# Two attentions: the products with the values move ahead of the projections in TensorE's order

## The reference, cut to what matters

```python
def cross_attention(x, ctx, wq, wk, wv, wo, bo):
    q = einsum('bne,ef->bnf', x, wq)      # 20 heads of 64
    k = einsum('bme,ef->bmf', ctx, wk)
    v = einsum('bme,ef->bmf', ctx, wv)
    scores = einsum('bhnd,bhmd->bhnm', q, k) * 64 ** -0.5
    attn = softmax(scores)
    out = einsum('bhnm,bhmd->bhnd', attn, v)
    return einsum('bnf,fe->bne', out, wo) + bo

x = cross_attention(layer_norm(x), layer_norm(x), ...) + x   # "self"
x = cross_attention(layer_norm(x), context, ...) + x         # "cross"
```

## Time and profile before

| | |
|---|---|
| median of 3 runs | 1538.18 us (1535.44 to 1538.56) |
| profiled execution, its own time | 1541.71 us |
| its span, first to last instruction | 1539.9 us |
| TensorE busy | 1384.9 us (90%) |
| DVE, ACT, POOL busy | 1077.4, 756.4, 723.1 us |
| mean granted TensorE clock | 0.959 of full speed |

### The profile page before, as it was taken

The page is one execution under the profiler, slowest core; times in us unless marked ns, Lnnn a source line. Parts: engine busy times, 40 slices in busy tenths (PEclk is TensorE's granted clock), DMA queues, the critical chain, the costliest instruction groups (busy, mean ns, idle before and its releaser), DMA issues. The chain is left out here.

```text
span 1539.9 us, 39601 instructions
## 1 busy us (share of the span) xinstructions
PE 1384.9 (90%) x16544; PEld 1183.2 (77%) x16544; DVE 1077.4 (70%) x2019; ACT 756.4 (49%) x1389; POOL 723.1 (47%) x514
## 2 busy tenths in 40 slices
PE   4697689997699999999979999999999999998587
PEld 3574477875588888888966888888888888887477
DVE  2774678884777778777647776767777777764476
ACT  0442357764355455554534555555555554544243
POOL 1242157675643344433433555555555554556154
PEclk9999889997799999999987999999999999999699
DMA  4110000000200000000010000000010000000000
GB/s 103 52 39 1 21 7 12 5 2 1 63 2 2 2 2 2 2 2 2 2 38 6 2 7 2 7 2 7 2 40 3 1 2 2 2 2 2 13 14 21
DMA packets 23484, 19.25 MB, mean 12 GB/s; under 512 B 12950, under 2 KB 21722, under 8 KB 23322
## 3 DMA queue, kind: packets, MB, share of 16 engines
q1 hardware_dynamic: 23322, 16.89, 4.1%
HBM read 15.57 MB, written 1.31 MB: 11 GB/s over the span
## 5 line engine op out<-in xcount | busy, mean ns | idle before, releaser
L492 POOL TENSOR_TENSOR cross_probs_l<-cross_probs 128x1024 f16<-128x1024 f32 x160 | 303.6, 1898 | 276.3 <-ACT cross_probs L563 276.0
L563 ACT ACTIVATE cross_probs<-cross_score 128x1024 f32<-128x1024 f32 x160 | 164.0, 1025 | 249.8 <-PE cross_score L805 249.8
L492 POOL TENSOR_TENSOR self_probs_l<-self_probs 128x1024 f16<-128x1024 f32 x80 | 151.5, 1894 | 204.1 <-ACT self_probs L563 203.7
L660 DVE TENSOR_REDUCE cross_maxima<-cross_max 128x2 f32<-128x1024 f32 x160 | 194.7, 1217 | 7.4 <-PE cross_max L781 7.2
L1971 POOL TENSOR_TENSOR ad_probs_l<-ad_probs 128x1024 f16<-128x1024 f32 x64 | 121.1, 1893 | 89.3 <-ACT ad_probs L2028 89.0
L563 ACT ACTIVATE self_probs<-self_score 128x1024 f32<-128x1024 f32 x80 | 82.3, 1028 | 156.7 <-PE self_score L805 156.7
L825 PEld LDWEIGHTS cross_pv<-cross_v_h,cross_probs 128*128 128x128 bf16 x1280 | 116.5, 98 | 33.2 <-issue 28.2
L825 PE MATMUL cross_pv<-cross_v_h,cross_probs 128*128 128x65 bf16 x1280 | 135.2, 196 | 2.6 <-POOL cross_probs_l L492 2.6
L646 DVE TENSOR_TENSOR cross_qk_l<-cross_shared,cross_qk_h 128x256 fp32r<-128x256 f32 (+1 forms) x160 | 87.9, 556 | 69.0 <-ACT cross_qk_h L548 68.8
L826 PE MATMUL cross_pv<-cross_v_l,cross_probs 128*128 128x64 f16 x1280 | 133.8, 194 | 0.0
L827 PE MATMUL cross_pv<-cross_v_h,cross_probs_l 128*128 128x65 bf16 x1280 | 133.4, 193 | 0.0
(11 more groups left out here) (439 smaller groups left out, 4806.6 us busy)
## 6 DMA issues: line engine op xcount, KB each, us to landing
ad_ctx_rows<-in_ctx SPq DMA_DIRECT2D x8, 192.0 KB, 2.5
cross_ctx_rows<-in_ctx SPq DMA_DIRECT2D x8, 192.0 KB, 2.7
x_rows<-in_x SPq DMA_DIRECT2D x1, 1280.0 KB, 6.9
sw_raw<-in_L_xattn_wq SPq DMA_DIRECT2D x2, 640.0 KB, 6.1
sw_raw<-in_L_xattn_wk SPq DMA_DIRECT2D x2, 640.0 KB, 3.5
sw_raw<-in_L_xattn_wv SPq DMA_DIRECT2D x2, 640.0 KB, 3.8
cw_raw<-in_L_xattn_wq SPq DMA_DIRECT2D x2, 640.0 KB, 4.1
lr_raw<-in_L_xattn_w_ff SPq DMA_DIRECT2D x2, 640.0 KB
```

What stands on the lines that cost most here:

```text
L492: nc.gpsimd.tensor_tensor(probs_l[:, n % PR, :, :].rearrange("p j k -> p (j k)"), whole, whole.bitcast(BF16)[:, 1::2], ALU.subtract).then_ ...
L563: nc.scalar.activation(probs[:, n % PR, :, :].rearrange("p j k -> p (j k)"), score_bank[:, :], ACT.Exp, scale=SCALE).then_inc(exped, 1)
L660: nc.vector.reduce_max(out, scores, AX.X).then_inc(max_read, 1)
```

## The change

It reorders one list. In each round the groups of `weigh` stand first, directly behind maxima and scores, and the shared items follow. Their own order, and so the ring of shared banks, the order on ACT, DVE and POOL, and every wait's count, stay as they are.

```diff
--- before.py
+++ after.py
@@ -319,18 +319,21 @@
         cur, more = kind != "tail", extras(kind, s)
         last = ROUNDS - 1
         out = []
+        weigh = (s >= WEIGH and cur) or (s < WEIGH and kind != "first")
+        if cross:
+            out += [(0, ("weigh", group)) for group in (0, 1) if weigh]
+        else:
+            out += [(0, ("weigh", group)) for group in range(4) if weigh]
         if (s >= MT and cur) or (s < MT and kind != "first"):
             out.append((0, ("mt", s)))
         out += [(0, key) for key in more[:2] if cross]
-        weigh = (s >= WEIGH and cur) or (s < WEIGH and kind != "first")
         if cross:
-            out += [(0, ("weigh", group)) for group in (0, 1) if weigh]
+            out += [(last, ("weigh", group)) for group in (2, 3) if weigh]
         if cur:
             out.append((last, ("proj", s)))
             if cross:
                 out.append((last, ("kproj", s)))
         out += [(last, key) for key in (more[2:] if cross else more)]
-        out += [(last, ("weigh", group)) for group in ((2, 3) if cross else range(4)) if weigh]
         return out
```

## The result

The changed kernel took 1655.49 us, the median of 4 runs (1651.77 to 1657.88), against 1538.37 (1535.44 to 1539.98, 4 runs) for the kernel before on the same chip. The ratio is 1.0761 [1.0736, 1.0787]. The forecast was 1659, so the time lies 3.5 us from it and on the side that was given 0.96.

What follows compares the result with a forecast made beforehand. TensorE's own order was taken as the bound (busy 47.3 of 48.1 us per self batch, 75.2 of 75.8 cross). Cross +60.7, self +62.0, changing kinds -2 gave 121: 1541.7 became 1663, less 3.5 hence 1659 us; range 1625 to 1695.

Steps and rivals of the forecast that it cites:

- The path: Last shared item on TensorE, ACT's cast, DVE's low part, reciprocal, multiplication, up to the multiplication's end: 2.28 us.
- The ordinary wait: In an ordinary slot of either attention, TensorE's next products wait 0.72 us for DVE's multiplication.
- The waits of cross: New TensorE waits summed over the cross-attention's slots: 64.3 us, 63 of them at 0.72.
- Slots with statistics: Slot 1, self and cross, statistics in front of the reciprocal: wait 1.52 us, six times in each attention.
- cross slot 4: Slot with `ln` work on ACT and DVE: 8.2 us against some 6.9 of TensorE's, wait 1.3, six times.
- the steady waits on maxima in cross fall away: Waits of 0.6 us in each of six cross batches, 3.6 in all, were to vanish.
- The waits of self: New TensorE waits summed over the self-attention's slots: 71.5 us, 35 of them at 0.72.
- Slot 3: Self slot with the normalisation on DVE: grows from 3.84 to 6.17 us, wait 2.33, six times.
- What goes: Old waits to vanish: cross maxima 3.6 us; self bank wait 4.0 and small stalls in slot 8 and at `ot` 5.5.
- Changing between kinds: TensorE's switches between matmul kinds, 240 rounds: products into a projection 0.08 us; together about -2 us, bounds -24 and +22.
- Rival 3: TensorE's clock falls at waits in self slots 3 and 4: 6 to 31 us more, middle 1675; chance 0.20.
- Rivals 1 and 2: First: no wait arises, order cheaper, 1525 us, chance 0.03; second: only slow slots pay, 1579 us, chance 0.05.

Runs made afterwards that it cites:

- x3: Changed kernel, but DVE does the reciprocal and multiplication right behind the slot's last reduction of maxima; 1532.78 us, ratio 0.9981 to the kernel before.
- x5: Changed kernel plus one unread DVE reduction in each slot ahead of the wait for `pv_done`; 1733.73 us, ratio 1.1281 to the kernel before.
- x6: Kernel before plus one unread DVE reduction in each slot ahead of the wait for `pv_done`; 1554.16 us, ratio 1.0114.
- cross alone: New order in the cross-attention only, self as in the kernel before; 1589.77 us, ratio 1.0354 to the kernel before.

## Why the prediction was right

**The mechanism.** It was that the last act of DVE's slot comes due earlier on TensorE while the path to it stays. x3 takes it off the path and with it the whole loss; x5 lengthens the path and pays 78 us of the 87 that 160 times 0.54 can be, where x6 pays 18. The hand-over of 0.15 us came out so in the slots shown (0.15, 0.16, 0.10). The path was right (2.29 against 2.28). The ordinary wait reads 0.67 us in the rows and not 0.72, since a row counts from the scores' modelled end, 1.44 us behind the maxima's start, and the forecast from the next instruction's start, 1.38 behind it. In time the forecast stands: the same cross slot lasts 7.77 us from product to product in x3, which has no wait (1000.13 to 1007.90), and 8.48 in after (1091.46 to 1099.94), 0.71 more.

**The signs** that the prediction named came out thus: a cross batch of 82.7 us for about 84, a self batch of 55.7 to 57.4 for about 57, the longest wait in self 2.3 for 2.4, idle time up by 110 us for some 120. The clock leaving 1.00 in the attentions was named as a sign of being wrong, and in self it did leave it; what that cost stands below.

**The waits of cross**, forecast at 64.3 us, were 54.1 (49.8 on DVE and 4.3 in the tail slots on POOL). Slots with statistics wait 1.46 (forecast 1.52). The term that failed is cross slot 4, "wait 1.3, six times" (its own terms, 2.4, 1.15 and 4.74, make 8.3 and not 8.2, so even 1.4), and with it "the steady waits on maxima in cross fall away". Timeline of the changed kernel, behind that slot:

```profile
1138.20 1.02 DVE L649 TENSOR_TENSOR cross_qk_l<-cross_shared,cross_qk_h 128x256 fp32r<-128x256 f32 x2
1138.31 0.49 PE L784 MATMUL cross_max<-cross_qk_h 64*128 64x512 f32 x2 [0.81 <-DVE cross_maxima L663]
```

I had laid these waits at the second maxima of slot 4. They are at the first maxima of slot 5, whose bank waits for the reduction that stands behind the `ln` work on DVE, and were 0.60 each before. So the delay of slot 4 is mostly paid there, where 0.60 was already being paid; the products behind it wait only 0.10. The forecast had 6 x (1.3 - 0.60) = 4.2 us for the two places together, and they cost 6 x (0.10 + 0.81 - 0.60) = 1.9. The total on maxima went from 6.7 to 8.3, where it was to fall by 3.6. The cross stage grew by 51.2 us where 60.7 were forecast (cross alone, by its median, 54.6). Slot 4 explains 2.3 of that. Idle time grew by 54.2 us, and TensorE's busy time in cross fell by 3.0; what the changes between kinds and the short spells of low clock at the stage's start have in this, no run takes apart.

**The waits of self**, forecast at 71.5, were 62.6. Slot 4 waits 2.29 (forecast 2.4). Slot 3 was mis-sized. Timeline of the changed kernel, self slots 3 and 4:

```profile
456.75 1.89 POOL L495 TENSOR_TENSOR self_probs_l<-self_probs 128x1024 f16<-128x1024 f32 x1 [3.26 <-ACT self_probs L566]
457.20 1.53 DVE L598 TENSOR_SCALAR self_xn<-x_rows,self_mean_var,self_rstd 128x128 f32<-128x128 f32 x1
...
459.48 0.33 DVE L598 TENSOR_SCALAR self_xn<-x_rows,self_mean_var,self_rstd 128x128 f32<-128x128 f32 x1
...
461.39 0.42 DVE L682 TENSOR_TENSOR self_attn<-self_pv,self_recip 128x256 f32<-128x256 f32 x1
...
461.97 0.19 PE L828 MATMUL self_pv<-self_v_h,self_probs 128*128 128x65 bf16 x1 [1.79 <-DVE self_attn L682]
...
468.13 0.21 PE L828 MATMUL self_pv<-self_v_h,self_probs 128*128 128x65 bf16 x1 [2.29 <-issue]
```

From multiplication to multiplication it was 6.17 us before and is 5.66 now (from 455.73 to 461.39), so the wait is 1.79 and not 2.33. The slots whose last item is `out` wait 0.10 to 0.12 where 0.25 was taken, and slot 8 waits 0.22 for 0.4. DVE's work is the same; only what it stood beside changed. The longest normalising step takes 1.53 us here and took 2.03 before, as less of POOL's split was left when it began.

**What goes** in self came in part. The bank wait of 4.0 us is no longer in the list, but of the other 5.5, which were an estimate, little shows. x3 has self batches shorter by 0.8 us than before, which is 5.6 in seven and not 9.5. And in after, the idle time in self grew by 57.0 us where the products' waits grew by 61.3 (62.6 against 1.3), so that 4.3 went, hardly more than the bank wait.

**Changing between kinds** was taken at 0.08 for products into a projection. Timeline of x3, which has after's order on TensorE:

```profile
1012.13 0.19 PE L834 MATMUL cross_pv<-cross_v_h,cross_probs_l 128*128 128x65 bf16 x1
1012.16 0.36 PE L760 MATMUL cross_shared<-cross_ln_h,cw_wq_h 128*128 128x256 f32 x1
1012.36 0.28 PE L760 MATMUL cross_shared<-cross_ln_l,cw_wq_h 128*128 128x256 f32 x1
1012.48 0.28 PE L760 MATMUL cross_shared<-cross_ln_h,cw_wq_l 128*128 128x256 f32 x1
```

The projection starts 0.03 behind the last product, and holds the next back for 0.20 where 0.12 is usual: 0.08, as taken. The Trainium skill, "TensorE: Matmul & The Clock Gate", "Part 2: What happens when you issue a matmul", prices a load of 128 columns at 107 ns. The 0.08 is near that in size, but that a load is its cause isn't shown: loads of 128 columns for the products, recorded at 0.10 us each, follow each other 0.03 us apart in the same rows.

```profile
1012.07 0.10 PEld L833 LDWEIGHTS cross_pv<-cross_v_l,cross_probs 128*128 128x128 bf16 x1
1012.10 0.10 PEld L834 LDWEIGHTS cross_pv<-cross_v_h,cross_probs_l 128*128 128x128 f16 x1
```

**Rival 3 held in part.** Windows of the changed kernel: the wait that self slot 4 causes and what follows, and the same two stretches three batches on:

```profile
464.40:467.80 3.40, 1.44 (x19) 1.19 (x18) 2.75 (x7) 2.20 (x4) 0.81 (x1) 1.00 0.00 0
467.80:471.20 3.40, 3.07 (x33) 3.10 (x34) 1.36 (x2) 0.37 (x1) 1.31 (x1) 0.51 0.00 0
636.40:639.80 3.40, 1.18 (x18) 0.92 (x16) 3.02 (x8) 1.93 (x3) 1.08 (x1) 1.00 0.00 0
639.80:643.20 3.40, 3.34 (x42) 2.94 (x42) 1.71 (x3) 1.45 (x3) 1.04 (x1) 1.00 0.00 0
```

TensorE is busy for 1.44 of 3.4 us and is then granted half its clock, 1.2 instead of 2.4 GHz, for some 3.4 us. In the later batch it is busy for only 1.18 of 3.4 and keeps the full clock. So the length of the wait alone doesn't say whether the clock falls. It fell four times in self's six batches with these waits, at 467.9, 519.1, 583.9 and 689.7 us (the second and the fourth time at the wait of slot 3), and a batch with a fall takes 57.2 us where one without takes 55.7: 1.5 us each, 6 in all, not the 16 that the rival's middle had. The Trainium skill, "TensorE: Matmul & The Clock Gate", section "HAM oscillation — how this bites in real kernels", tells of a kernel in which the recurring wait put the clock down every time. Its waits are longer than any here, so it bore on this rival less than the prediction had it. Here two of the six waits went without a fall, and the steady cross batch shown is at 1.00 throughout.

So the closeness of the total is luck in part. In self the waits came out 9 us shorter than forecast, and two terms gave that back: stalls that were to go and stayed, some 5 us, and the clock, which the sum had left out, with 6. The stage grew by 61.3 us for a forecast of 62.0. In cross nothing made up for the shortfall, 51.2 against 60.7. The stages together grew by 112.5 us for a forecast of 121, and the medians lie 117.1 apart: the adapter in front of them, the same code in all, takes from 379 to 389 us in the profiled executions of this record. A scatter of that size helped to bring the result to within 3.5 us of the forecast. Rivals 1 and 2 are out: time was lost, and the product waits in ordinary slots (68 waits in cross).

## What to carry to other kernels

When work is moved forward on the bound engine, look at what empties the buffer it writes, and at what stands in front of that on the emptying engine; here, that engine's last act hung on the bound engine's own last result, and moving the producer alone turned 2.3 us of hidden latency into waiting in some 130 slots, mostly 0.67 us and at most 2.3. Move consumer and producer together (x3), or neither. And lengthen the suspected path by a known amount in both orders (x5, x6): if it is paid nearly in full in the one and hardly in the other, the path is the cause and not the load.

## What the runs showed of the hardware that was not expected

A normalising step of DVE between SBUF tiles takes 0.33 us alone. Beside POOL's split it takes as long as that split still runs, in each of the six batches that have it: in the rows of self slot 3 above, the split ends at 458.64, and the step that began at 457.20 ends at 458.73. The Trainium skill, "SBUF — State Buffer", section "SBUF: two separate sides", calls the pair of ports that the two engines share an exclusive lock, held for a whole instruction, for which the other one fully blocks. An end 0.09 us behind the split's fits that; which ports the step takes, no run shows. A mean duration of such a step contains this waiting and is no measure of its work.

The mean granted clock of a run says little here. The changed kernel's is 0.921 against 0.959, but most of that lies in the adapter, which the change doesn't touch. The same stretch in the window of after, then of before:

```profile
41.00:165.00 124.00, 93.06 (x678) 68.57 (x677) 82.73 (x177) 46.44 (x126) 40.70 (x49) 0.53 0.11 34
```

```profile
41.00:165.00 124.00, 94.56 (x678) 69.80 (x678) 83.01 (x178) 46.59 (x126) 40.25 (x49) 1.00 0.11 34
```

678 matmuls in 124 us at a granted 0.53, and 678 at 1.00, with no more busy time. In x3 the adapter's low clock is much the same (a mean of 0.80 up to its end, against 0.78 in after and 0.94 before), and x3 is no slower than before. What the low reading means in that stretch stays open; these windows show no cost of it.
